# The attention output projections of a four-layer kernel as three fp16 products of split halves in place of one f32 product

## What is computed

```python
x = L0(x, t)        # silu(scale * layernorm + shift) @ W_in, once more with W_out, + x; whole-item layernorm
x = L1(x, ...)      # adaLN; attention of 16 heads with a bias and a mask; x + (ctx @ Wo + bo)
                    # h = ln(x) * g2 + beta2;  x + gelu2(h @ W1 + b1) @ W2 + b2
x = L2(x, ...)      # a stencil of first and second differences, then max(., 0)
x = L3(x, gate)     # causal attention of 16 heads: x1 = x + (ctx @ Wo + bo)
                    # x2 = x1 + gelu(ln(x1) @ W1 + b1) @ W2 + b2;  x + g * (x2 - x)
```

## Time and profile before

| | us |
|---|---|
| device time, three runs | 2570.64, 2571.6, 2572.56 (median 2571.6) |
| the profiled execution, device time | 2576.85 |
| its span (first to last instruction) | 2575.5 |
| PE busy | 2455.6 (95%) |
| PE's weight loads | 2003.3 (78%) |
| ACT busy | 2110.1 (82%) |
| DVE busy | 1977.3 (77%) |
| POOL busy | 1539.3 (60%) |

### The profile page before, as it was taken

How to read it: one execution, slowest core, us unless ns; L and a number is a source line. 1 busy time by engine, 2 the same in 40 slices (tenths; PEclk the granted TensorE clock), 3 DMA queues, 4 the chain that set the end, 5 groups by cost and what they waited for, 6 DMA issues and landing times.

```text
span 2575.5 us, 57162 instructions
## 1 busy us (share of the span) xinstructions
PE 2455.6 (95%) x19136; PEld 2003.3 (78%) x19136; DVE 1977.3 (77%) x7387; ACT 2110.1 (82%) x4694; POOL 1539.3 (60%) x1487
## 2 busy tenths in 40 slices
PE   6878999999999999999999999999999999999997
PEld 5666788888878888887888888788888888877776
DVE  6776777888787787878778887877888787778653
ACT  2556888888888888888888888888888888888775
POOL 2556665655766665576666557666565766655421
PEclk6799999999999999999999999999999999999999
DMA  5433444434444443344444343444434344433311
GB/s 207 122 120 102 122 120 119 114 101 109 110 126 121 120 112 104 107 108 126 121 122 111 105 109 105 126 122 122 111 103 112 103 126 122 128 103 98 84 30 34
DMA packets 141667, 287.58 MB, mean 112 GB/s; under 512 B 33792, under 2 KB 37888, under 8 KB 141120
## 3 DMA queue, kind: packets, MB, share of 16 engines
q1 hardware_dynamic: 141376, 283.92, 40.1%
HBM read 174.64 MB, written 8.45 MB: 71 GB/s over the span
## 4 chain that ended last, share of the span: by engine, by line
PE 78%; ACT 11%; DVE 5%; POOL 3%; issue 2%; DMA 1%; SPq 1%; POOLq 0%; DVEq 0%; ACTq 0%
PE bank L1452 18%; PE bank L1530 17%; PE bank L1553 11%; PE bank L1568 7%; PE bank L1512 7%; PE bank L1543 6%; ACT PB L1254 4%; PE bank L1464 3%; PE bank L1519 3%; PE bank L1706 2%; PE bank L1578 2%; ACT BB L1274 1%; ACT AA L1280 1%; ACT BB L1280 1%; DVE smt L989 1%
## 5 line engine op out<-in xcount | busy, mean ns | idle before, releaser
L1254 ACT ACTIVATE PB<-PB,mx 128x256 f32<-128x256 f32 (+1 forms) x2048 | 844.1, 476 | 35.8 <-DVE mx L1011 34.7
L580 POOL TENSOR_TENSOR BT<-BT,MN 128x1024 f32<-128x1024 f32 x256 | 555.9, 2185 | 74.4 <-DMA BT<-in_bias 73.8
L1553 PE MATMUL bank<-ident,PB 128*128 128x128 f32 x3584 | 483.6, 274 | 6.9 <-ACT PT L1259 3.2
L1011 DVE CUSTOM_DVE_ANT_0 PB<-bank,BT 128x256 f32<-128x256 f32 x1024 | 373.3, 420 | 122.1 <-PE bank L1543 118.2
L1553 PEld LDWEIGHTS bank<-ident,PB 128*128 128x128 f32 x3584 | 421.2, 141 | 57.9 <-ACT PB L1254 11.5
L1452 PE MATMUL bank<-TN,WS_w 128*128 128x256 f16 x3072 | 379.9, 274 | 42.7 <-ACT BB L1280 22.8
L1018 DVE COPY PT<-bank 128x512 f32<-128x512 f32 (+1 forms) x512 | 316.1, 617 | 89.3 <-PE bank L1553 89.1
L1452 PEld LDWEIGHTS bank<-TN,WS_w 128*128 128x128 f16 x3072 | 286.0, 98 | 122.9 <-ACT AA L1280 39.7
L1543 PE MATMUL bank<-Ks,Qs 96*128 96x512 f32 (+1 forms) x1024 | 359.6, 428 | 13.9 <-DVE mx L1011 8.6
L1011 DVE CUSTOM_DVE_ANT_0 PB<-bank,caus 128x128 f32<-128x128 f32 (+1 forms) x1024 | 303.3, 352 | 69.9 <-PE bank L1543 69.7
L1259 ACT ACTIVATE PT<-bank 128x512 f32<-128x512 f32 (+1 forms) x512 | 272.7, 533 | 72.8 <-PE bank L1553 72.8
(11 more groups left out here) (282 smaller groups left out, 4654.8 us busy)
## 6 DMA issues: line engine op xcount, KB each, us to landing
BT<-in_bias SPq DMA_DIRECT2D x256, 512.0 KB, 4.5
Qs<-QX SPq DMA_DIRECT2D x256, 128.0 KB, 2.7
Ks<-KX SPq DMA_DIRECT2D x512, 64.0 KB, 2.4
Qs<-QX SPq DMA_DIRECT2D x256, 64.0 KB, 2.6
Ks<-KX SPq DMA_DIRECT2D x512, 32.0 KB, 2.2
XT<-in_xT SPq DMA_DIRECT2D x32, 256.0 KB, 5.2
X<-in_x SPq DMA_DIRECT2D x32, 256.0 KB, 3.0
AB<-ada_rows SPq DMA_DIRECT2D x32, 256.0 KB, 3.8
```

What stands on the lines that cost most here:

```text
L580: G.op.tensor_tensor(v2(BT[k % 4]), v2(BT[k % 4]), MN[:, :].unsqueeze(1).broadcast_to([128, 2, 512]), ALU.add).then_inc(g_bt, 1)
L1011: V.op.tensor_tensor_reduce(PB[(2 * D + q) % 6][:, h * 256:h * 256 + w], bS[q][:, h * w:h * w + w], plus, -1.0, 3.0e38, ALU.add, ALU.min, ...
L1254: S.op.activation(o, o, ACT.Exp, scale=-1.0, bias=mx[u.layer][:, c:c + 1]).then_inc(a_exp, 1)
L1553: last = T.op.transpose(bP[h][:, c * 128:c * 128 + 128], PB[(2 * u.D + q) % 6][:, h * 256 + k * 128:h * 256 + k * 128 + 128], ident[:, :])
```

## The change

Both `o1` and `o3` become `split_N` with weights from a new fp16 buffer `WN` (128 by 2048). `c1_out` and `c3_out` write the high half only, and two new pieces, `c1_lo` and `c3_lo`, write the low half on DVE (`rest`, a tensor_tensor that subtracts the high half from the bank). The products wait for these pieces rather than for ACT's copy. Since weights and values carry scales, the adds of `m1` and `m4` multiply the bank by a factor of one value per partition and so become scalar_tensor_tensor. `o1` and `o3` are no longer loaded to `Wf`. New pieces `split_wn`, `split_wn_hi` and `split_wn_lo` in item 0 load them to `CX[1]` and `CX[3]` and split them: two DMAs, two row maxima and nine more instructions on DVE, two on ACT, a transpose and a matmul on PE. Five small DVE instructions are added to the splits of p1 and p3, whose scales now serve the ones column of V too. `w2` and `w4` stay f32. All due ticks in `P`, `OWN` and `SPLIT` are other numbers.

```diff
-SQUARE = {n: 4096 + 512 * i for i, n in enumerate(("W_in", "W_out", "o1", "o3"))}
+SQUARE = {n: 4096 + 512 * i for i, n in enumerate(("W_in", "W_out"))}
+SECOND = {"o1": (0, 1, 9216), "o3": (1024, 1, 9728)}
...
-    "score0": -1, "score1": -1, "bias0": 0, "bias1": 0, "exp0": 2, "exp1": 3, "flip0": 8, "flip1": 8, "ev0": 7,
+    "score0": -2, "score1": -1, "bias0": -1, "bias1": 0, "exp0": 2, "exp1": 3, "flip0": 8, "flip1": 8, "ev0": 9,
...
+    "c1_lo": 48, "c3_lo": 48, "split_wn": -21, "split_wn_hi": -20, "split_wn_lo": -19,
...
-            square(d_sq, "o1", "o3")
...
+                for b in at(t, "split_wn"):
+                    if b == 0:
+                        S.wait_ge(p_set, 5)
+                        S.wait_ge(v_ws, made("p3"))
+                        S.wait_ge(p_ws, 3)
+                        S.wait_ge(v_cf, 25)
+                        for n, c, raw in staged():
+                            a = SECOND[n][2] + 512 * c
+                            S.op.dma_start(raw[:, :], A["wf"][:, a:a + 512]).then_inc(d_wn, 16)
...
+            def second_max():
+                V.wait_ge(d_wn, 32)
+                for i, (n, c, raw) in enumerate(staged()):
+                    V.op.tensor_reduce(an[:, i:i + 1], raw[:, :], AX.X, ALU.max, apply_absolute_value=True).then_inc(v_wn, 1)
...
+            def second_rest():
+                for i, (n, c, raw) in enumerate(staged()):
+                    V.wait_ge(a_wn, i + 1)
+                    V.op.scalar_tensor_tensor(out=second(n, c, True), in0=raw[:, :], scalar=gain_of(n), in1=second(n, c),
+                                              op0=ALU.mult, op1=ALU.subtract).then_inc(v_wn, 1)
...
+                for b in at(t, "c1_lo"):
+                    V.wait_ge(a_c1, b + 1)
+                    rest(MC, bM, v_c1)
                 for b in at(t, "m1"):
                     x = X[b % 5]
+                    V.wait_ge(v_wn, SECOND_MADE)
                     V.wait_ge(p_o1, b + 1)
                     V.wait_ge(g_x1, 7 * b + 7)
-                    V.op.tensor_tensor(x[:, :], bM[:, :], x[:, :], ALU.add).then_inc(v_m1, 1)
+                    V.op.scalar_tensor_tensor(out=x[:, :], in0=bM[:, :], scalar=unscale_of("o1"), in1=x[:, :], op0=ALU.mult,
+                                              op1=ALU.add).then_inc(v_m1, 1)
...
+                for b in at(t, "c3_lo"):
+                    V.wait_ge(a_c3, b + 1)
+                    rest(turned(b), tail_bank(b), v_c3)
...
-                    S.op.activation(MC[:, :], bM[:, :], ACT.Copy).then_inc(a_c1, 1)
+                    S.wait_ge(v_wn, SECOND_MADE)
+                    S.op.activation(hi(MC), bM[:, :], ACT.Copy).then_inc(a_c1, 1)
...
-                    S.op.activation(turned(b)[:, :], tail_bank(b)[:, :], ACT.Copy).then_inc(a_c3, 1)
+                    S.op.activation(hi(turned(b)), tail_bank(b)[:, :], ACT.Copy).then_inc(a_c3, 1)
...
                 for b in at(t, "o1"):
-                    T.wait_ge(d_sq, 16)
-                    T.wait_ge(a_c1, b + 1)
-                    lin_N(bM, "o1", MC).then_inc(p_o1, 1)
+                    T.wait_ge(v_wn, SECOND_MADE)
+                    T.wait_ge(v_c1, b + 1)
+                    split_N(bM, WN, 512, SECOND["o1"][0], MC).then_inc(p_o1, 1)
...
                 for b in at(t, "o3"):
-                    T.wait_ge(a_c3, b + 1)
-                    lin_N(tail_bank(b), "o3", turned(b)).then_inc(p_o3, 1)
+                    T.wait_ge(v_c3, b + 1)
+                    split_N(tail_bank(b), WN, 512, SECOND["o3"][0], turned(b)).then_inc(p_o3, 1)
```

More of the change, by code:

```diff
@@ L166 @@
 SPLIT = {
[L167 to L168 removed]
+    "bias1_3": 1, "exp0_3": 3, "exp1_3": 3, "ev0_3": 8, "ev1_3": 10, "pv_3": 13, "cx_3": 13, "ct_3": 16, "pvn_3": 18,
+    "stack_3": -16,
 }
@@ L362, in made, with staged, second, gain_of @@
         def made(n):
-            steps = {"w1": 21, "p3": 31, "w3": 21}
+            steps = {"w1": 21, "p3": 34, "w3": 21}
             return sum(steps[m] for m in ORDER[:ORDER.index(n)])
+        def staged():
+            return [("o1", 0, CX[1]), ("o3", 0, CX[3])]
+        def second(n, c, rest=False):
+            a, k, _ = SECOND[n]
+            z = a + (512 * k if rest else 0) + 512 * c
+            return WN[:, z:z + 512]
+        def gain_of(n):
+            i = list(SECOND).index(n)
+            return wn[:, 4 + i:5 + i]
+        def unscale_of(n):
+            return {"o1": wn[:, 9:10], "o3": scale_of("p3", 7)}[n]
+        SECOND_MADE = 11
         def raw1(i):
@@ L1184, in tail @@
                     rest(TN, tail_bank(b), v_t4)
+                for b in at(t, "c3_lo"):
+                    V.wait_ge(a_c3, b + 1)
+                    rest(turned(b), tail_bank(b), v_c3)
                 for b in at(t, "m4"):
                     y = Y3[b % 2]
+                    V.wait_ge(v_ws, made("w3"))
                     V.wait_ge(p_o3, b + 1)
                     V.wait_ge(g_m3, 5 * b + 5)
-                    V.op.tensor_tensor(y[:, :], tail_bank(b)[:, :], y[:, :], ALU.add).then_inc(v_t, 1)
+                    V.op.scalar_tensor_tensor(out=y[:, :], in0=tail_bank(b)[:, :], scalar=unscale_of("o3"), in1=y[:, :],
+                                              op0=ALU.mult, op1=ALU.add).then_inc(v_t, 1)
                     V.wait_ge(v_t, 5 * b + 1)
@@ L1224, in vector @@
                         first_rest()
+                for b in at(t, "split_wn"):
+                    if b == 0:
+                        second_max()
+                for b in at(t, "split_wn_hi"):
+                    if b == 0:
+                        second_gains()
+                for b in at(t, "split_wn_lo"):
+                    if b == 0:
+                        second_rest()
                 for n in ORDER:
@@ L1313, in scalar @@
                             S.op.activation(first_hi(i), raw1(i), ACT.Identity, scale=wp[:, 10 + i:11 + i]).then_inc(a_p1, 1)
+                for b in at(t, "split_wn_lo"):
+                    if b == 0:
+                        S.wait_ge(v_wn, 7)
+                        for n, c, raw in staged():
+                            S.op.activation(second(n, c), raw[:, :], ACT.Identity, scale=gain_of(n)).then_inc(a_wn, 1)
                 for n in ORDER:
@@ L1487, in split_spread, with second_turn, second_spread @@
                 T.op.matmul(ps[:, 128:129], ones[0:1, :], am[0:1, 9:10], start=True, stop=True).then_inc(p_ws, 1)
+            def second_turn():
+                T.wait_ge(v_wn, 2)
+                T.op.transpose(bT_[0:2, 0:128], an[:, 0:2], ident[:, :]).then_inc(p_wn, 1)
+            def second_spread():
+                T.wait_ge(v_wn, 5)
+                T.op.matmul(bT_[:, 128:130], ones[0:2, :], an[0:2, 8:10], start=True, stop=True).then_inc(p_wn, 1)
             def split_bias(n):
@@ L1620, in tensor @@
                         first_spread()
+                for b in at(t, "split_wn"):
+                    if b == 0:
+                        second_turn()
+                for b in at(t, "split_wn_hi"):
+                    if b == 0:
+                        second_spread()
                 for n in ORDER:
```

81 lines of the change are left out of this document (58 added, 23 removed), and 136 rows, old and new, of tables (OWN, P).

## The result

The changed kernel takes 2585.03 us (median of four runs, 2583.61 to 2589.54) against 2571.12 for the kernel before (2568.28 to 2572.56): ratio 1.0053, 95% interval 1.0035 to 1.0071. It is slower by 13.9 us, beyond what the prediction called no change. The range 2554 to 2587 holds it; the likeliest value, 2572, is 13 us too low. The profiled execution took 2589.54 us with a span of 2588.2, 12.7 above the span of before. Medians and ratios here are of fast runs alone; one run of the kernel before beside e1 to e4, 2842.32 us at a granted clock of 0.839, is not among them.

A forecast was written before the change was run, and what follows sets the result against it. PE was taken as the bound nearly everywhere, with 32 items pacing the run. Steady part 0.00, start 0 and end +0.5 on the profiled 2576.85 gave 2577.4, less 5.2 to the median: 2572 us, 8-in-10 range 2554 to 2587.

The forecast's parts named there:

- The product: Each projection on PE, as 12 fp16 matmuls: 1.52 us instead of 1.95, or 0.41 less from start to start.
- layer 1: Projection o1: PE waits 0.59 us for DVE's low half; less the 0.41 saved, the item loses 0.18 us.
- Layer 3: Projection o3: wait of 0.2 to 0.3 us for the low half, product ends as before; +0.06 us an item.
- The recurring waits: PE's once-an-item waits ahead of w3 (0.72 us) and w1 (0.58): -0.24 us an item at w3, 0 at w1.
- sum of the steady part: Per item, 0.18 + 0.06 - 0.24 + 0 = 0.00 us, about +-0.3.
- the stacks: Stacked Q and K loads in SP's rearranged queue, issued earlier for layer 3: taken as 0, since no recurring PE wait names them.
- The start: Splitting the o1 and o3 weights puts the first score at 92 against 84.94, +7 us; 0 of it at the end.
- (B): Rival: the start's +7 us are never made up behind it, 2579 us; chance 0.15.
- The end: Last two items of layer 3: the low half is on the path, +0.26 us each, +0.5 in all.
- (A): Rival: the low half's wait is hidden and PE's saving arrives, 2546 us in full, 2559 if half; chance 0.31.
- (C): Rival: the low half stands behind biases in DVE's queue, +0.3 us an item, 2582, or 2589 with (B); chance 0.11.
- (D): Rival: the two further waits before the products bring PE's clock down to 0.95, +124 us, 2697; chance 0.02.

The follow-up runs named there:

- e1: The changed kernel with score0 due at -1 instead of -2, so the two scores of a unit stand side by side again; 2607.5 us, ratio 1.0136.
- e4: The changed kernel without the low-half pieces c1_lo and c3_lo, its 12 matmuls reading the high half in their place; 2584.5 us, ratio 1.0049.
- g2: The kernel before (f32 projections, no split weights, no low halves) with the order tables of the changed kernel; 2598.6 us, ratio 1.0098.
- g3: The changed kernel with layer 1's projection moved behind the product with V and K's product one tick later, in middle items; 2592.0 us, ratio 1.0080.
- e3: The changed kernel with the order tables of the kernel before, layer 3's low half due at tick 49, not 48; 2681.2 us, ratio 1.0420.

## Why the prediction was right or wrong

**The product** and the wait in **layer 1** were right: 1.50 against 1.52 us, 1.41 from start to start, +0.17 against +0.18 at the piece behind. The wait for the low half is as worked out, 0.58 against 0.59, marked as 0.40. At `t2` 0.12 of it are left.

**Layer 3** was right in its sum, +0.06, and wrong in what makes it. (Its two terms, 0.05 later and an add 0.06 longer, give 0.11 as they stand.) I had a wait of 0.2 to 0.3 for the low half and a product that ends as before. There is none; the moved score takes its place. g2 shows that the new order costs 0.49 there and that the split gives 0.43 back.

**The recurring waits** were over-rated: -0.24 at w3 became -0.11 (from w3's first group to `c1`, 25.80 against 25.91). The third slot was taken as 2.42 and is 2.52, since PE's own work fills it: a group 1.23, the moved score 0.29, PV 1.00.

```profile
1228.22 1.47 PE L1556 MATMUL bank<-TN,WS_w 128*128 128x256 f16 x12
1229.45 0.36 PE L1659 MATMUL bank<-Ks,Qs 96*128 96x256 f32 x1
1229.74 1.07 PE L1684 MATMUL bank<-PT,VW 128*32 128x256 f32 x16
1230.74 1.48 PE L1556 MATMUL bank<-TN,WS_w 128*128 128x256 f16 x12
```

What I took as 0 from `t2` to `c3` became +0.23, and g2 shows that all of it comes with the order. Some 0.2 can be named: w2 starts 0.44 after the turn of the last context half instead of 0.26, behind a gelu. So the step that failed is the sum of the steady part: 0.00 became +0.28 in a quiet period, inside the +-0.3 that stood beside it. The prediction saw the new order mainly as a gain at w3, -0.24; by itself the order costs 0.62 an item (g2). And it took the split as a loss of 0.18 + 0.06 at the two products, where it gives 0.33 back.

**Left out altogether** were the stacks. I took SP's rearranged queue as nothing, because no recurring wait of PE named it. In the new order the score reads its stack one piece sooner, and the stack was freed by an earlier score. Kernel after, PE, then SP:

```profile
1332.77 0.48 PE L1659 MATMUL bank<-Ks,Qs 96*128 96x512 f32 x1
...
1340.01 0.50 PE L1659 MATMUL bank<-Ks,Qs 96*128 96x512 f32 x1 [0.55 <-DMA Ks<-KX]
```
```profile
1333.56 0.59 SPq L517 DMA_DIRECT2D Qs<-QX  x1
...
1336.74 0.59 SPq L523 DMA_DIRECT2D Ks<-KX  x1
```

Score, six issues, landing, score: this loop just fits, and in some items it doesn't. Here the last load lands 3.2 us after its issue; in the quiet item before it (issue 1261.90) it took 2.0, and the score starts at 1263.95, 0.05 after the landing. The marked waits for stacks are 3.5 us of the 4.8 of irregular time over 23 periods, against none before.

**The start** was near in size (5.9 at the first score against 7), by luck, since the stacks on which the 7 hung had landed 3.5 us before the score. It was wrong in what becomes of it. I took 0 of it at the end. It was 6.15 at the first `c1` and 8.2 at the tenth turn, and the line of PE-paced items behind it gives nothing back: rival (B) as it stood. g2, with no weights to split, has its first `c1` at 118.27 and its tenth turn at 524.90, 0.3 ahead of the kernel before. So the order costs nothing at the start, and the delay comes with the split; which of its pieces makes it was not taken apart (e4, without low halves, still has 4.3 at the tenth turn). **The end** was wrong too: from the turn at 2270.49 on, the last items give 6.4 us back where I had +0.5. g2, with the same tables, gives back only 1.4 (322.7 us from its turn at 2274.46, against 324.1 before and 317.7 in the changed kernel). No run took this apart.

**The rivals.** (A), the hidden wait, was not what happened, and g3 and e4 show that in this order it couldn't have paid: 0.1 us an item is all that lies there. The argument for it, "work taken from PE is worth its full time if nothing else is late", left out what else is late, K's eviction, done 3.4 us behind the product's end (1240.95 to 1244.36). (B) happened, and decided the sign together with the steady +0.28 and the stacks. (C) didn't happen in this order: the low half starts 0.03 after ACT's copy, so the sign that I had set for a period of 75.3 or more, a start over 0.1 late, failed. The period came out longer for another reason, the order. In e3 the mechanism of (C) makes a wait of 2.5 us an item. (D) didn't: the clock of the period is 1.00, and so it is from 455 to 2400 us, with the waits at the products in it. The Trainium skill, "TensorE: Matmul & The Clock Gate", section "A second HAM failure mode: psum-queue depth-cycling", tells of another kernel whose clock swung with short idle times between groups of matmuls; this trace doesn't show that.

The chances gave "slower" 0.28 and "same" 0.39. That 2585 lies in the range, 2 us from its end, is partly luck: the end's 6.4 us, which nothing in the prediction foresaw, cancel a third of the 19.1 us of delay that had come up before. The sums at the two products were good to 0.02 us; the one at w3 was 0.13 off, and the larger misses are in what I had set to 0 by default.

## To carry to other kernels

Where engines work in fixed orders that were tuned together, ask of a shorter instruction not only whether its engine is the bound but what the next wait behind it is, also one that ends just in time and so shows no idle time; follow each engine's queue to the next point where it is met. A new instruction on an engine with 23% of idle time may still find no gap at its place, and making one can move the loss elsewhere. Ask also what a new order costs by itself: here a run with the old code in the new order told the 24 us of the order from the 12 that the split gives. Every term set to 0 because "no wait names it" needs its slack read from the trace: here landing times of loads against the first use.
